# A state-space mixer beside three other layers on one core: one bank for its row broadcasts, a later start of its scan, and an earlier turn of the gate weights

## What is computed

```
x = x + L0_attn(ln(x))   # bidirectional state-space scan (Mamba), 256 channels, 16 states
x = x + L0_ffn(ln(x))    # 16 experts of 64, 2 of them kept by groups, plus shared ones
x = x + L1_attn(ln(x));  x = x + L1_ffn(ln(x))
x = x + L2_attn(ln(x));  x = x + L2_ffn(ln(x))   # attention, layer norm, 8 experts of 512 with gelu
x = x + L3_attn(ln(x));  x = x + L3_ffn(ln(x))   # memory scan; 8 experts of 256 with silu and a gate
```

```
h = exp(delta[d] * A[d, n]) * h + (delta[d] * x[d]) * B[n]
y[d] = sum over n of h[n] * C[n]
```

## Time and profile before

| | us |
|---|---|
| median of three runs | 5807.86 |
| the profiled execution, its own time | 5812.37 |
| its span in the trace | 5810.6 |
| stage first | 165.7 |
| each of the seven slots | 316.8 to 316.9 |
| the last slot, without a mixer | 181.3 |

### The profile page before, as it was taken

One profiled execution on the slowest core, in us unless ns is written; L12 is line 12 of the kernel. 1 busy time (PEld: TensorE's weight loads), 2 busy tenths in 40 slices (PEclk: granted clock), 3 DMA queues, 4 the chain that ended last, 5 costly groups with the idle time before them and its releaser, 6 DMA issues. The chain is left out here.

```text
span 5810.6 us, 67170 instructions
## 1 busy us (share of the span) xinstructions
PE 4485.7 (77%) x20516; PEld 2226.2 (38%) x20516; DVE 3772.0 (65%) x8877; ACT 3064.0 (53%) x5351; POOL 1140.3 (20%) x1356
## 2 busy tenths in 40 slices
PE   5786778877788777887778777788778877788777
PEld 2342434424344243442434324343243433444334
DVE  6756586565865658656686556865668555686554
ACT  3365645556455555555655556555565555555443
POOL 2401132011320123201231012310123111231100
PEclk8996989978898788987889878897789987899778
DMA  4210021100210002100121001210012100121000
GB/s 160 87 36 1 21 65 55 32 1 25 67 55 26 1 28 71 52 22 1 34 73 47 20 1 37 75 48 13 1 42 75 46 11 1 44 73 47 7 1 2
DMA packets 104076, 218.53 MB, mean 38 GB/s; under 512 B 11072, under 2 KB 19776, under 8 KB 103152
## 3 DMA queue, kind: packets, MB, share of 16 engines
q1 hardware_dynamic: 103680, 213.81, 11.6%
HBM read 211.08 MB, written 2.69 MB: 37 GB/s over the span
## 5 line engine op out<-in xcount | busy, mean ns | idle before, releaser
L859 POOL TENSOR_TENSOR slot_work<-slot_work,slot_c_all 128x512 f32<-128x512 f32 x448 | 570.2, 1273 | 1015.9 <-DVE slot_work L942 1015.0
L777 PE MATMUL BANKS<-slot_work,WF 128*128 128x512 f32 x896 | 530.5, 679 | 5.7 <-DVE slot_du L918 2.9
L524 ACT ACTIVATE attn_prob<-BANKS 128x512 f32<-128x512 f32 (+3 forms) x896 | 401.5, 532 | 122.5 <-PE BANKS L426 119.0
L1000 PEld LDWEIGHTS BANKS<-WF,slot_x_a 128*128 128x128 f32 x2688 | 359.3, 197 | 264.5 <-ACT slot_x_a L1040 133.5
L1000 PE MATMUL BANKS<-WF,slot_x_a 128*128 128x128 f32 x2688 | 373.3, 283 | 86.3 <-ACT slot_x_a L1040 86.3
L1010 PE MATMUL BANKS<-XT,WF 128*128 128x512 f32 x768 | 425.3, 639 | 2.6 <-ACT slot_comb_t L306 2.6
L769 PE MATMUL BANKS<-slot_bcs,WB 96*128 96x512 bf16 x448 | 189.1, 422 | 305.1 <-DVE slot_work L942 304.0
L202 POOL TENSOR_TENSOR rstd<-rstd,WF 128x4 f32<-128x4 f32 x40 | 40.3, 1007 | 1572.7 <-DVE rstd L220 1559.5
L1809 DVE CUSTOM_DVE_ANT_0 attn_biased<-BANKS,attn_toep 128x512 f32<-128x512 f32 x448 | 306.0, 684 | 51.9 <-PE BANKS L1707 46.6
L1788 ACT COPY attn_probt<-BANKS 128x512 f32<-128x512 f32 x448 | 261.0, 583 | 147.3 <-PE BANKS L1714 144.4
L426 PE MATMUL BANKS<-attn_parts_kT,attn_parts_qT 64*128 64x512 bf16 (+3 forms) x896 | 309.2, 437 | 33.6 <-ACT attn_parts_qT L504 20.7
(11 more groups left out here) (674 smaller groups left out, 9464.7 us busy)
## 6 DMA issues: line engine op xcount, KB each, us to landing
slot_c_all<-c_rows SPq DMA_DIRECT2D x448, 256.0 KB, 3.1
attn_toep<-bias_line SPq DMA_DIRECT2D x112, 448.0 KB, 4.4
first_c_all<-c_rows SPq DMA_DIRECT2D x64, 256.0 KB, 3.1
WF<-in_wf SPq DMA_DIRECT2D x4, 1964.0 KB, 16.2
zattn_toep<-bias_line SPq DMA_DIRECT2D x16, 448.0 KB, 4.3
WF<-in_wf SPq DMA_DIRECT2D x3, 800.0 KB, 17.2
WF<-in_wf SPq DMA_DIRECT2D x3, 785.5 KB, 6.0
XIN<-in_x SPq DMA_DIRECT2D x8, 256.0 KB, 2.9
```

The lines of the kernel that those rows point to most:

```text
L524: nc.scalar.activation(prob[:, i % PR, lo:hi], bank("T", i), ACT.Exp).then_inc(exped, 1)
L777: nc.tensor.matmul(SUM, ident, work[:, m % RW, :], start=(n == 0), stop=(n == NS - 1)).then_inc(acc, 1)
L859: nc.gpsimd.tensor_tensor(work[:, m % RW, :], work[:, m % RW, :], c_all[:, m % RC, :], ALU.mult).then_inc(rd, 1)
L1000: last = nc.tensor.matmul(DOWN[e % 2][:, j * D:(j + 1) * D], a1[:, i % 3, j * P:(j + 1) * P], w_down[:, i * D:(i + 1) * D], start=(t == 0 ...
```

## The change

Four things are changed.

1. The banks of the scan step: TensorE now always spreads into one bank, `SPREAD = PS[3]`, and waits for multiplication `s - 1` (semaphore `drv`) where it waited for scan `s - 3`. VectorE multiplies out of it into `DRIVE[s % 2]`. In TensorE's plan the spread of step `s` stands one `STEP` later than before, so that the place which held spread `s` now holds spread `s - 1`; the sums keep their places (`AHEAD` counts one less).
2. `SCAN` goes from 52.0 to 70.0. All places of the scan, on all engines, come 18 planned us later against `last_layers`, which is about seven steps.
3. On ScalarE the line `yield 28.4` ahead of the copies `dt_rows(0)` and `bc_rows(0)` is taken out: they now follow the two silus of direction 0 at once.
4. The turn of the gate weights stands after half of the tiles, not three quarters.

```diff
--- before.py
+++ after.py
@@ -670,7 +670,7 @@
 
         STEPS = 2 * ND * NS
         RD, RW, RC, AHEAD, FLUSH = 5, 8, 3, 5, 4
-        PRE, SCAN, STEP = 13.5, 52.0, 2.6
+        PRE, SCAN, STEP = 13.5, 70.0, 2.6
         TAIL = SCAN + STEP * STEPS
         zs = st.sb("zs", [P, ND, SEQ])
         xc = st.sb("xc", [P, 2, ND, SEQ])
@@ -702,7 +702,7 @@
         b_cast, dec, drv, scn, rd, acc = (st.sem(n) for n in ("b_cast", "dec", "drv", "scn", "multiplied", "acc"))
         yev, dud, emptied, ych, outp = (st.sem(n) for n in ("yev", "du_done", "emptied", "ych", "outp"))
         c_ld = [st.sem(f"c_ld{i}") for i in range(RC)]
-        SUM, DRIVE, OUT = PS[0], (PS[1], PS[2], PS[3]), PS[1]
+        DRIVE, SPREAD, SUM, OUT = (PS[1], PS[2]), PS[3], PS[0], PS[1]
 
         def step(i):
 
@@ -755,23 +755,26 @@
                     last = nc.tensor.matmul(PS[2 + t][:, :], W("dt_T", DTR + 1)[:, i * P:(i + 1) * P],
                                             dts[:, d, :], start=True, stop=True)
                 last.then_inc(dpr, 1)
-            for s in range(STEPS + AHEAD + 1):
+            for s in range(STEPS + AHEAD):
                 if s < STEPS:
                     d, _, n = step(s)
-                    yield SCAN + STEP * (s - 1) - 0.9
+                    yield SCAN + STEP * s - 0.9
+                    if s % (ND * NS) == 0:
+                        pe.wait_ge(sc, 5 * (d + 1))
                     if s == 0:
-                        pe.wait_ge(sc, 10)
                         pe.wait_ge(relued, 2)
                         pe.wait_ge(crows, 2)
-                    if s >= 3:
-                        pe.wait_ge(scn, s - 2)
+                    else:
+                        pe.wait_ge(drv, s)
                     row = WBF("pick", 96)[:, n:n + 1]
-                    nc.tensor.matmul(DRIVE[s % 3], bc(row, [96, P]), bcs[:, d, :], start=True, stop=True).then_inc(b_cast, 1)
-                m = s - AHEAD - 1
+                    nc.tensor.matmul(SPREAD, bc(row, [96, P]), bcs[:, d, :], start=True, stop=True).then_inc(b_cast, 1)
+                m = s - AHEAD
                 if m >= 0:
                     n = m % NS
-                    yield SCAN + STEP * (s - 1) + 0.2
+                    yield SCAN + STEP * s + 0.2
                     pe.wait_ge(rd, m + 1)
+                    if m == 0:
+                        pe.wait_ge(sc, 10)
                     if n == 0 and m:
                         pe.wait_ge(emptied, m // NS)
                     nc.tensor.matmul(SUM, ident, work[:, m % RW, :], start=(n == 0), stop=(n == NS - 1)).then_inc(acc, 1)
@@ -811,7 +814,6 @@
                     act.wait_ge(conved, d * ND + t + 1)
                     nc.scalar.activation(xc[:, d, t, :], xc[:, d, t, :], ACT.Silu).then_inc(silu, 1)
                 if d == 0:
-                    yield 28.4
                     dt_rows(0)
                     bc_rows(0)
             yield 36.0
@@ -932,14 +934,18 @@
                     dve.wait_ge(b_cast, s + 1)
                     if s % (ND * NS) == 0:
                         dve.wait_ge(dud, d + 1)
-                    V.tensor_tensor(DRIVE[s % 3], DRIVE[s % 3], du[:, d, t, :], ALU.mult).then_inc(drv, 1)
+                    if s == 0:
+                        dve.wait_ge(relued, 2)
+                    if s >= 2:
+                        dve.wait_ge(scn, s - 1)
+                    V.tensor_tensor(DRIVE[s % 2], SPREAD, du[:, d, t, :], ALU.mult).then_inc(drv, 1)
                 m = s - 1
                 if m >= 0:
                     dve.wait_ge(drv, m + 1)
                     dve.wait_ge(dec, m + 1)
                     if m >= RW:
                         dve.wait_ge(acc, m - RW + 1)
-                    V.tensor_tensor_scan(work[:, m % RW, :], decay[m % RD], DRIVE[m % 3], 0.0,
+                    V.tensor_tensor_scan(work[:, m % RW, :], decay[m % RD], DRIVE[m % 2], 0.0,
                                          ALU.mult, ALU.add).then_inc(scn, 1)
                 if s >= NS and s % NS == FLUSH:
                     flush(s // NS - 1)
@@ -960,7 +966,6 @@
     def experts_parts(st, tag, gate, ready, w_up, w_gate, b_up, b_gate, w_down, b_down, E, tiles_per, comb, comb_t, acc, at, step):
 
         n = E * tiles_per
-        TURN = 3 * n // 4
         both = w_gate is not None
         UP, DOWN = (PS[4], PS[5]), (PS[6], PS[7])
         a1 = st.sb(f"{tag}_a1", [P, 3, SEQ])
@@ -971,7 +976,7 @@
 
         ring = []
         for i in range(n):
-            ring += [("up", i)] + [("gate", i)] * both + [("turn", 0)] * (i == TURN)
+            ring += [("up", i)] + [("gate", i)] * both + [("turn", 0)] * (i == n // 2)
         ring.append(("bias", 0))
         slot = {item: k for k, item in enumerate(ring)}
 
@@ -1015,7 +1020,7 @@
                 if i >= 1:
                     yield at + 0.2 + step * (i + 0.5)
                     down(i - 1)
-                if i == TURN:
+                if i == n // 2:
                     gate.turn(pe, place("turn", 0))
             yield at + 0.2 + step * n
             pe.wait_ge(gate.moved, 1)
@@ -1031,7 +1036,7 @@
             gate.exponents(act)
             for i in range(n):
                 yield at + 0.2 + step * i + 1.0
-                if i == TURN + 1:
+                if i == n // 2 + 1:
                     gate.move(act, UP[slot["turn", 0] % 2])
                 if not both:
                     act.wait_ge(hid, i + 1)
```

## The result

The changed kernel takes 5853.24 us (median of 4 runs, 5848.54 to 5857.81) against 5807.78 (5805.65 to 5812.37) for the kernel before: ratio 1.008, 95% interval 1.0065 to 1.0093. It is slower, as forecast, 17 us above the 5836 predicted and inside the range. Its profiled execution took 5859.19, with a span of 5857.5.

What follows compares the result with a forecast made beforehand. VectorE was taken to bound the memory layer and lone mixer, TensorE the first experts, no engine the second. +3.95 us a slot, 27.7 for seven, plus 0.7 gave +28.4: 5836 us, own range 5820 to 5850, whole range 5796 to 5884.

Steps and rivals of the forecast that it cites:

- Start of the slot: Before the softplus block's end: TensorE stands 2.8 us for a gelu behind ScalarE's copies; 2.6 carried on.
- First experts: First experts in a slot, seven scan steps less done beside them: −3.0 us.
- Norms and projections: Stretch after the first experts: spread 6 stands behind the projections, so VectorE reaches their results later: +1.65 us.
- the memory layer: Up to its first step +0.3 us; in it −1.4; norm and first gate tiles −0.3.
- Second experts: Spreads wait only for the multiplication; twelve tiles at 4.95 us plus 2.4: −6.0; last tile +0.5.
- The end: Last scan begins 14.1 us after the last gate product, +13.4; from it to the mixer's last addition −1.2.
- The slot: Sum of the terms for one slot: +3.95 us, 27.7 for seven equal slots.
- Stage first: Mixer alone: second spread waits once for the first multiplication, +0.7 us; steps stay at 1.73.
- 1 (one bank too few): VectorE and TensorE take turns in the second experts, tiles 5.65 or gain eaten: 5878 us; chance 0.16.
- 2: Seven steps leaving the first experts give −8 there, memory layer all 4.2: slot −3.9, 5781 us; chance 0.17.
- 3: Terms cancel: half of the faster early part's gain, within 0.2% of before; chance 0.17.
- 4: The 2.8 us stall early in the slot lowers TensorE's clock: +2.5 us a slot, 5854 us; chance 0.08.

Runs made afterwards that it cites:

- e9: Kernel before with only the `yield 28.4` ahead of ScalarE's copies taken out; 5831 us, ratio 1.0036.
- e7: Changed kernel with the `yield 28.4` ahead of ScalarE's two copies put back; 5809 us, ratio 0.9996 to the kernel before.
- e3: Kernel before with only `SCAN` moved from 52.0 to 70.0; 5786 us, ratio 0.9958.
- e2: Kernel before, its three banks and waits kept, with each spread one `STEP` later in TensorE's order; 5759 us, ratio 0.9916.
- e4: Changed kernel with a third product bank in the stage first alone; 5839 us, ratio 1.0053 to the kernel before.
- e11: Kernel before with the later places of e2 and `SCAN` at 57.2; 5743 us, ratio 0.9884.
- e1: Changed kernel with `SCAN` 52.0, the yield and the turn's place as before, leaving the bank scheme; 5828 us, ratio 1.0028 to the kernel before.
- e10: Kernel before with the later places of e2 and `SCAN` at 70.0; 5794 us, ratio 0.9971.
- e5: Kernel before with only `SCAN` moved from 52.0 to 51.8; 5784 us, ratio 0.9954.
- e6: Kernel before with the later places of e2 and `SCAN` at 51.8; 5816 us, ratio 1.0013.
- e12: Kernel before with the later places of e2 and `SCAN` at 62.4; 5784 us, ratio 0.9956.

## Why the prediction came out as it did

- **Start of the slot: right.** The stall is 2.66 us (forecast 2.8), the restart behind the softplus block at 66.9 us of the slot (forecast 66.8). But the whole price of edit 3 is 4.1 to 4.9 us a slot (e9, e7), more than the 2.6 carried.
- **First experts: −2.3** against −3.0 (103.7 against 106.0). By e3 the later start alone gives −6.5, and without edit 3 it is −6.0 (e7), so edit 3 took nearly all the rest back.
- **Norms and projections: +2.7** against +1.65: the wait for spread 6 is there. By e2 (+2.2) and e3 (0.0) it comes with the later places. Up to the memory layer +0.8 (+0.3), in it −1.4 (−1.4), for the norm and the first gate tiles −1.3 (−0.3). The exact hit in the memory layer is luck in part: slot 1 has −3.0 there with the same instructions.
- **Second experts: −5.3** for twelve tiles against −6.0, 5.21 us each; the last tile −0.2 against +0.5. The size is right, the reason incomplete: the waits for scans went, as said, but e2 and e3 remove them without the bank. The prediction credited the new bank with what the new order did.
- **The end: +14.1** against +13.4. The 0.7 more is in the four multiplications of the six that have a scan right ahead of them: 1.92 us a step in place of 1.73. From the last scan to the last addition −1.2 (−1.2).
- **The slot:** for slot 3 these make +5.9; the seven sum to +32.0, or +4.6 each, against +3.95. Slot 1 has a higher granted clock (0.88) than slot 3 (0.85) for the same instructions and is 4.5 us shorter, 4.4 of them ahead of gate product 2; why is open. In before the seven were alike, so the forecast took one for seven:

```profile
628.87:947.13 318.26, 244.12 (x912) 130.72 (x912) 237.65 (x397) 173.99 (x215) 93.27 (x74) 0.88 0.17 54
2069.10:2391.88 322.78, 249.41 (x912) 134.25 (x912) 237.83 (x397) 174.09 (x215) 93.19 (x74) 0.85 0.17 53
```

- **Stage first: the step that failed.** That "its steps stay at VectorE's 1.73, since a spread (0.5) fits beside a scan (1.2)" priced TensorE's side of the new wait and left out VectorE's: +12.2 in place of +0.7, and most of the 17 us missed. e4 shows the wait: 11.6 us between the scans.
- **Rivals.** 1 (one bank too few) fell for the slots, where multiplications wait for spreads 1.3 us in twelve tiles, though with the wait for the scan the scheme costs 4.3 us a slot next to e2. 2 fell for the changed kernel, but its mechanism, seven steps less beside the first experts, is real in e3. 3 fell, as the slots are 4.6 us longer. 4 fell in its place: behind the stall the clock stays at 1.00. The down group there takes 1.16 us against 1.05, but so does one in e11 with nothing idle ahead of it (at 911.74).

```profile
663.70:670.00 6.30, 6.24 (x29) 3.75 (x30) 1.52 (x4) 3.67 (x6) 0.00 (x0) 1.00 0.00 0
```

The total came out nearer than its parts, which is luck. Asked for them one by one after the result, the theory gave 5781 us for edit 1 alone (e1, measured 5828) and about 5860 for edit 2 alone (e3, measured 5786). These errors, 47 and 74 us, have opposite signs, and the total does not show them.

The account of the change by its parts, per slot: later start and places −4.1 (e10), one bank and the turn +3.7 (e7 − e10), copies +4.9 (after − e7), together +4.5. What helps is the order; the bank scheme and the copies cost more than it gives.

**Still open:** why the first experts end 3.6 to 3.8 us later with the start at 51.8 (e5, e6); how much of e11's gain is the flush that falls elsewhere; and whether a start between those run with the later places (51.8, 52.0, 57.2, 62.4, 70.0) is better than 57.2.

## What to carry to other kernels

Price a new wait on the side that waits, even if it is for the instruction right ahead on the same engine: here it cost 0.19 us in each step. When an edit changes resources and order together, run the order alone first; here it held the whole gain. Where two streams are merged by planned times, try shifts by whole steps and by a small part of one: with the later places, starts from 51.8 to 70.0 gave medians from 5743 to 5816 us, more than any of the four edits moved. And run the parts of a change even when its total came out as forecast, since errors in the terms can cancel.

## What the runs showed of the hardware

- A multiplication with a wait for the scan directly ahead of it on VectorE starts 1.31 us after that scan's start; without it 1.12, while the scan is listed at 1.21. So this pair overlaps by 0.1 us by its listed times, and the semaphore puts 0.1 us between them (stage first of after, e4 and before).
- After TensorE's idling of 2.45 us at the end of e12, two sums took 3.53 us (a sum is 0.86 at full clock), and the granted clock of the stretch is 0.69. After 2.66 us of idling early in after's slot 1 the granted clock stayed at 1.00.
